# Narrow diagonal blocks share a bank in the max pass of a two-layer causal attention kernel

## The chip, the cores and the metric

The kernel runs on one core of a Trainium2 chip. The metric is the device time of one execution in microseconds (us), as the median of several runs. A core has a matrix engine (TensorE, PE in the rows), a vector engine (VectorE, DVE), an activation engine (ScalarE, ACT), GpSimd (POOL) and SyncE (SP), which work side by side and meet at semaphores. Matrix results land in PSUM, which has eight banks of 128 partitions by 512 fp32 values.

## What is computed

Two transformer layers in "macaron" form over x of 2048 tokens by 128 features, all fp32. Each layer is half an FFN, a causal attention, and the same half FFN again. The change touches the attention alone, of which there are two:

```
x = x + 0.5 * L0_ffn(layernorm(x))     # 8 experts, top 1, then a layernorm
x = x + L0_attn(layernorm(x))          # 16 heads of 8, with output projection
x = x + 0.5 * L0_ffn(layernorm(x))
x = x + 0.5 * L1_ffn(layernorm(x))     # ternary weights, relu
x = x + L1_attn(layernorm(x))          # 16 heads of 8, no output projection
x = x + 0.5 * L1_ffn(layernorm(x))

scores = einsum('bhqd,bhkd->bhqk', q, k)
scores = where(causal, scores, -inf)
attn   = softmax(scores / sqrt(8), axis=-1)
ctx    = einsum('bhqk,bhkd->bhqd', attn, v)
```

## The kernel before

**Steps and turns.** The 16 heads are taken in four groups `g` of four (`G`), the 2048 queries in four chunks `c` of 512 (`CH`). A step `(g, c)` is one group with one chunk. The 16 steps of a layer (`STEPS`) go up with groups 0 and 1, (0,0), (1,0), (0,1), ... (1,3), and down with groups 2 and 3, (2,3), (3,3), (2,2), ... (3,0). A step has 4(c+1) *quads*: four heads, 128 keys (block `j`), up to 512 queries. The last four quads of a step are *diagonal*: their queries begin at the key block, so they are 512, 384, 256 and 128 wide, and a mask is added to their first 128 columns. One quad, with some work of the max pass beside it, is a *turn*; a layer has 160 turns with a quad, 64 of them diagonal.

**The two passes.** The softmax needs each query's maximum before the exponent is taken, and the maximum is put into the score product as an added row of `q_slots`. So there is a max pass two steps ahead (`AHEAD = 2`). Its *units* are scores with queries on the partitions: block `i` of 128 queries of the chunk, key chunk `kc`, one head. TensorE multiplies (L1202), and where `kc == c` adds a causal mask on the last 128 columns (L1205). A unit with `kc < c` is 512 columns wide, one with `kc == c` (i+1)·128. VectorE takes its maximum from the bank (L1317). Units go through a ring of three PSUM banks (`RING = 3`): TensorE waits on `ring_read` for unit n-3 before unit n, and VectorE waits on `ring_full`. When a step's units are all read, VectorE joins their maxima (L1361, `neg_max`), a turn later TensorE turns them (L1210), VectorE splits them in two halves (L1334, L1336), and a DMA puts them into `q_slots`.

**One quad.** TensorE makes two score tiles of two heads each (`score_tile`, L1162, 32 rows of the array per head, four heads on four different sets of rows). Tile 0 of a quad uses the first pair of banks and tile 1 the second, so each waits for the exponent of the same tile of the quad before. In a diagonal quad two mask products (L1169) follow in each tile, on all 128 rows. ScalarE takes the exponent of a tile (L1279). One turn later TensorE multiplies with the values of the four heads (`values`, L1182, fp32, four heads on four sets of columns). The sum over a step stands in one bank, `O_BANK`; ScalarE copies it out (L1287) after the step's last values, and the next step's first values wait for that copy. Two turns later TensorE turns the result (L1225) and VectorE divides (L1344, L1348).

**The order of a turn.** It is written out in code, with `cuts = [0, 0, len(items) // 2 + len(items) // 4, len(items)]`: the quad's two score tiles, the first part of the turn's ring items (3 of 4, 1 of 3), the values of the quad before, the rest of the items. The items are units and the late work (`max`, `out`, `turned`, `project`), in that order.

**How units are dealt.** `units_beside_quads` weighs each unit as `UNIT_FIXED` plus its columns, each quad as `QUAD_FIXED` plus its columns, and gives each turn what the most pressing deadline asks. The deadline of a step's units is `SLACK = 3` turns before the step starts. The units of the first two steps run ahead of all quads.

## Time and profile before

| | us |
|---|---|
| median of 3 runs | 1314.45 (1314.13 to 1315.17) |
| the profiled execution, its time | 1314.37 |
| the profiled execution, its span | 1312.6 |
| layer 0's attention, first score tile to last values | about 203 to 643 |
| layer 1's attention | about 851 to 1280 |
| TensorE busy, whole span | 1186.3 (90%) |
| VectorE busy | 1033.5 (79%) |
| ScalarE busy | 668.8 (51%) |

The page divides the span of one execution by engine, by time and by group of instructions. "L1317" is a line of the kernel. An idle time with an arrow names what ended it. The matrix engine's rows overlap: a product of 512 columns has a row of 0.39 us, and the next one starts 0.22 us after it. So a busy TensorE isn't one at its limit, and how long a thing holds it is read from one start to the next in the timeline.

### The profile page before, as it was taken

The numbers are of one execution on the slowest core, as the hardware profiler recorded it, in microseconds if no ns is written. First come the engines' busy times: TensorE is split into PE (matmuls) and PEld (weight loads), VectorE is DVE, ScalarE is ACT, GpSimd is POOL, SyncE is SP. The second block draws the span as 40 slices with busy tenths as digits, with TensorE's granted clock in tenths as the row PEclk, the third lists the DMA queues.
The fourth block names the chain that finished last, engine by engine and source line by source line (L and its number), as shares of the span: only waits on it lengthen the run. The fifth ranks groups of instructions, "written<-read, shape, count | busy, mean of one in ns | idle before, by whom it ended". The sixth has DMA issues, their size and how long they took to land.

```text
span 1312.6 us, 21461 instructions
## 1 busy us (share of the span) xinstructions
PE 1186.3 (90%) x8293; PEld 461.7 (35%) x8293; DVE 1033.5 (79%) x2503; ACT 668.8 (51%) x861; POOL 65.3 (5%) x62
## 2 busy tenths in 40 slices
PE   1899968999999999999699979599999999999997
PEld 1455533222222222333355547232222222222336
DVE  8976487899999897875547566789999999877664
ACT  1322114555677667766332224145556667777663
POOL 5111010000000000000101000100000000000000
PEclk9999988999999999999799979799999999999999
DMA  4100141000000000000000000420000000000001
GB/s 147 33 1 1 48 121 57 1 2 1 2 1 1 2 1 1 1 1 2 1 0 1 1 0 25 146 57 1 1 2 1 1 1 1 1 1 2 1 2 33
DMA packets 23506, 23.26 MB, mean 18 GB/s; under 512 B 3134, under 2 KB 21220, under 8 KB 23404
## 3 DMA queue, kind: packets, MB, share of 16 engines
q1 hardware_dynamic: 22252, 18.73, 4.9%
q0 software_dynamic: 1152, 3.15, 0.9%
q8 instruction: 66, 1.08, 0.3%
q14 instruction: 36, 0.29, 0.1%
HBM read 13.20 MB, written 8.39 MB: 16 GB/s over the span
## 4 chain that ended last, share of the span: by engine, by line
PE 69%; DVE 25%; issue 2%; ACT 2%; DMA 1%; SPq 0%; DVEq 0%; ACTq 0%
PE psum L1182 19%; PE psum L1202 17%; DVE part_max L1317 14%; PE psum L442 9%; PE psum L1162 8%; PE psum L1169 4%; PE psum L466 2%; PE psum L898 2%; PE psum L1205 2%; PE psum L913 1%; DVE xn L167 1%; DVE norm_v L150 1%; PE psum L427 1%; DVE parts L838 1%; PE psum L1225 1%
## 5 line engine op out<-in xcount | busy, mean ns | idle before, releaser
L1317 DVE TENSOR_REDUCE part_max<-psum 128x1 f32<-128x512 f32 (+3 forms) x1280 | 703.5, 604 | 118.2 <-PE psum L1205 59.4
L1279 ACT ACTIVATE hidden<-psum 128x1024 f32<-128x1024 f32 (+3 forms) x640 | 542.4, 895 | 311.1 <-PE psum L1169 166.1
L1202 PE MATMUL psum<-k_slots,q_slots 128*128 128x512 f16 (+3 forms) x1280 | 396.8, 359 | 43.5 <-DVE part_max L1317 24.4
L1182 PE MATMUL psum<-hidden,v_aug 128*9 128x512 f32 (+3 forms) x2560 | 296.1, 535 | 0.0
L1202 PEld LDWEIGHTS psum<-k_slots,q_slots 128*128 128x128 f16 x1280 | 111.5, 97 | 402.0 <-DVE part_max L1317 320.0
L442 PE MATMUL psum<-parts,w_parts 128*128 128x512 f16 x768 | 177.6, 382 | 1.9 <-DVE parts L838 1.9
L1162 PE MATMUL psum<-q_slots,k_slots 32*128 32x512 f16 (+3 forms) x1280 | 163.9, 355 | 7.2 <-ACT hidden L1279 4.6
L1205 PE MATMUL psum<-ident_bf,later_keys 128*128 128x128 bf16 x512 | 111.0, 227 | 0.0
L442 PEld LDWEIGHTS psum<-parts,w_parts 128*128 128x128 f16 x768 | 73.2, 99 | 80.9 <-issue 3.0
L586 ACT CAST parts<-psum 128x512 f16<-128x512 f32 x64 | 37.2, 588 | 106.7 <-PE psum L427 106.7
L1162 PEld LDWEIGHTS psum<-q_slots,k_slots 32*128 32x128 f16 x1280 | 46.3, 91 | 109.4 <-issue 52.1
L1169 PE MATMUL psum<-later_keys,ident_bf 128*128 128x128 bf16 x512 | 73.8, 226 | 0.0
L1182 PEld LDWEIGHTS psum<-hidden,v_aug 128*9 128x9 f32 x2560 | 38.1, 88 | 72.3 <-issue 49.3
L838 DVE TENSOR_TENSOR parts<-parts 128x1024 f16<-128x1024 f16 x64 | 45.7, 738 | 18.3 <-ACT parts L586 18.2
L1205 PEld LDWEIGHTS psum<-ident_bf,later_keys 128*128 128x128 bf16 x512 | 51.9, 101 | 3.3 <-issue 0.3
L1169 PEld LDWEIGHTS psum<-later_keys,ident_bf 128*128 128x128 bf16 x512 | 29.2, 97 | 38.8 <-issue 27.1
L624 POOL TENSOR_TENSOR x_plus<-xn,bo_bc 128x512 f32<-128x512 f32 x8 | 13.8, 1720 | 566.1 <-DVE xn L167 527.4
L466 PE MATMUL psum<-wo_sb,hidden 128*128 128x128 f32 x256 | 33.3, 294 | 3.7 <-ACT hidden L577 3.7
L466 PEld LDWEIGHTS psum<-wo_sb,hidden 128*128 128x128 f32 x256 | 32.9, 209 | 5.6 <-ACT hidden L577 4.7
L953 POOL TENSOR_TENSOR x_plus<-x_res,fb_half 128x512 f32<-128x512 f32 x8 | 10.0, 1265 | 495.6 <-DVE xn L167 495.6
L244 ACT COPY xn_t<-psum 128x512 f32<-128x512 f32 x8 | 4.7, 587 | 58.2 <-PE psum L219 58.2
L675 DVE TENSOR_TENSOR x_plus<-psum,x_plus 128x512 f32<-128x512 f32 x8 | 5.5, 690 | 35.4 <-PE psum L466 35.4
(168 smaller groups left out, 735.7 us busy)
## 6 DMA issues: line engine op xcount, KB each, us to landing
q_slots<-q_rows SPq DMA_DIRECT2D x8, 512.0 KB, 3.8
k_slots<-k_rows POOLq DMA_DIRECT2D x24, 128.0 KB, 4.1
q_rows<-parts SPq DMA_DIRECT2D x18, 128.0 KB, 2.7
k_rows<-parts SPq DMA_DIRECT2D x18, 128.0 KB, 2.4
q_slots<-in_L_ffn_W_dram SPq DMA_DIRECT2D x2, 1024.0 KB, 6.6
k_slots<-k_rows SPq DMA_DIRECT2D x8, 128.0 KB, 4.0
q_slots<-nm_parts SPq DMA_DIRECT2D x64, 4.0 KB
out_dram<-x_res SPq DMA_DIRECT2D x4, 256.0 KB, 2.3
```

The source lines that it names most:

```text
L442: last = pe.matmul(psum[:, t, :], w1_parts[:, e, wp, t * P:(t + 1) * P], x_mask[:, k % NX, xp, :], start=(e == 0 and (wp, xp) == (0, 0)), ...
L466: last = pe.matmul(psum[:, DOWN_BANK, i * D:(i + 1) * D], hidden[:, n % 2, t, i * P:(i + 1) * P], wo2_sb[:, t, :], start=(t == 0), stop=(t ...
L586: act.copy(mask_sb[:, k % NX, :], psum[:, MASK_BANKS + k % 2, :]).then_inc(mask_ready, 1)
L838: dve.tensor_tensor(x_mask[:, k % NX, :, :], x_parts[:, n % 2, :, :], mask_sb[:, k % NX, :].rearrange("p (a t) -> p a t", a=1).broadcast_t ...
L898: last = pe.matmul(psum[:, 6 + n % 2, i * D:(i + 1) * D], hidden[:, n % 2, t, i * P:(i + 1) * P], tw2_t[:, t, :], start=(t == 0), stop=(t ...
L1162: last = pe.matmul(psum[:, S_BANKS + 2 * (tile % 2) + par, off:CH], k_slots[rows, G * g + 2 * pr + par, j * P:(j + 1) * P], q_slots[rows, ...
L1169: last = pe.matmul(psum[:, S_BANKS + 2 * (tile % 2) + par, off:off + P], ident_bf[:, :], later_keys[:, :], start=False, stop=True)
L1182: last = pe.matmul(psum[VW * h:VW * h + DH + 1, O_BANK, off:CH], v_aug[:, j, G * g + h, :], probs[:, (2 * n + h // 2) % NP, h % 2, off:CH] ...
L1202: last = pe.matmul(psum[:, bank, 0:w], q_slots[:, g, qb * P:(qb + 1) * P], k_slots[:, G * g + h, kc * CH:kc * CH + w], start=True, stop=kc ...
L1205: last = pe.matmul(psum[:, bank, i * P:w], later_keys[:, :], ident_bf[:, :], start=False, stop=True)
L1279: act.activation(probs[:, tile % NP, :, off:CH], psum[:, bank:bank + 2, off:CH], ACT.Exp, scale=scale).then_inc(exp_done, 1)
L1317: dve.tensor_reduce(dst, psum[:, bank, 0:w], axis=AX.X, op=ALU.max).then_inc(ring_read, 1)
```

## The change

Four things are done to both attentions.

1. **Units of several heads.** Where a diagonal unit is 128 wide, all four heads go side by side into one bank, and where it is 256 wide, two heads. There are then as many products as before, but one mask product for the bank (its moving operand is the identity repeated, 512 or 2x128 columns), one signal, and one maximum of VectorE with 4 or 2 results. A step has 1 + 2 + 4 + 4 = 11 diagonal units where it had 16. The units of 384 and 512 columns stay as they are.
2. **Score tiles and masks.** In a diagonal quad the four score products of both tiles come first (`score_tile`), and then the four mask products (`mask_tile`), where each tile had its masks behind it. Tile 0 is now signalled only behind tile 1's products, which still wait for the exponent of tile 1 of the quad before.
3. **The cut.** A turn's items stand half ahead of the values (rounded up) and half behind.
4. **The weights.** `UNIT_FIXED` and `QUAD_FIXED` go from 64 and 64 to 100 and 500, and a unit's columns now count its mask. The units per turn that follow, of each step:

| step | turns before | turns after |
|---|---|---|
| (0,0) | 10 8 5 3 | 7 6 5 4 |
| (1,0) | 6 5 5 2 | 5 5 4 3 |
| (0,1) | 7 7 6 5 8 4 3 3 | 6 5 5 5 4 5 4 3 |
| (1,1) | 6 6 5 5 5 4 4 3 | 5 5 5 5 5 5 4 3 |
| (0,2) | 5 7 5 6 5 5 5 5 6 5 3 2 | 4 5 5 5 5 4 5 5 4 4 4 3 |
| (1,2) | 5 6 5 4 5 4 4 4 4 4 3 2 | 4 4 4 4 4 4 4 4 4 4 3 3 |
| (0,3) | 7 4 4 5 5 4 4 5 4 4 4 4 4 4 3 2 | 4 4 4 4 4 4 4 4 4 4 4 4 4 4 3 3 |
| (1,3) | 6 4 4 6 4 4 4 5 4 4 4 4 4 3 2 2 | 4 4 3 4 4 4 4 4 4 4 4 4 4 4 2 3 |
| (2,3) | 6 4 4 6 4 4 4 4 4 4 4 4 4 3 5 2 | 4 4 3 4 4 4 4 4 4 4 3 4 4 2 3 2 |
| (3,3) | 4 5 4 4 4 3 3 3 3 3 3 5 4 3 2 2 | 3 3 4 4 4 4 3 3 4 3 3 3 3 3 3 2 |
| (2,2) | 4 3 3 4 3 3 3 3 3 5 2 1 | 3 3 3 3 3 3 3 3 3 2 2 2 |
| (3,2) | 5 3 4 4 3 3 3 6 3 4 2 1 | 3 3 3 3 3 3 3 2 2 3 2 2 |
| (2,1) | 3 3 3 3 6 3 2 1 | 3 3 2 2 2 2 2 1 |
| (3,1) | 2 2 5 4 3 2 1 1 | 2 2 2 2 2 1 1 1 |
| (2,0), (3,0) | none | none |

The diff, cut to its core:

```diff
-        UNIT_FIXED, QUAD_FIXED = 64, 64
+        UNIT_FIXED, QUAD_FIXED = 100, 500
+                for kc in range(step[1] + 1):
+                    heads = CH // unit_width(step, i, kc)
+                    units += [(step, i, kc, h, heads) for h in range(0, G, heads)]
+            return heads * (unit_width(step, i, kc) + (P if kc == step[1] else 0))
...
-                    if q in diagonal:
-                        for par in range(2):
-                            last = pe.matmul(psum[:, S_BANKS + 2 * (tile % 2) + par, off:off + P],
-                                             ident_bf[:, :], later_keys[:, :], start=False, stop=True)
+                    if q not in diagonal:
+                        last.then_inc(scores_done, 1)
+                def mask_tile(q, pr):
+                    off = first_query(q)
+                    tile = 2 * quad_no[q] + pr
+                    for par in range(2):
+                        last = pe.matmul(psum[:, S_BANKS + 2 * (tile % 2) + par, off:off + P],
+                                         ident_bf[:, :], later_keys[:, :], start=False, stop=True)
                     last.then_inc(scores_done, 1)
...
-                        last = pe.matmul(psum[:, bank, 0:w], q_slots[:, g, qb * P:(qb + 1) * P],
-                                         k_slots[:, G * g + h, kc * CH:kc * CH + w], start=True, stop=kc < c)
+                        for a in range(heads):
+                            last = pe.matmul(psum[:, bank, a * w:(a + 1) * w], q_slots[:, g, qb * P:(qb + 1) * P],
+                                             k_slots[:, G * g + h0 + a, kc * CH:kc * CH + w],
+                                             start=(a == 0), stop=(kc < c))
                         if kc == c:
-                            last = pe.matmul(psum[:, bank, i * P:w], later_keys[:, :], ident_bf[:, :],
-                                             start=False, stop=True)
+                            last = pe.matmul(diagonal_part(psum[:, bank, 0:heads * w], heads),
+                                             later_keys[:, :], repeated(ident_bf, heads), start=False, stop=True)
...
-                    cuts = [0, 0, len(items) // 2 + len(items) // 4, len(items)]
+                    half = (len(items) + 1) // 2
                     if q:
                         score_tile(q, 0)
                         score_tile(q, 1)
+                    if q in diagonal:
+                        mask_tile(q, 0)
+                        mask_tile(q, 1)
+                    for item in items[:half]:
                         ring_item(item)
                     if previous:
                         values(previous)
+                    for item in items[half:]:
                         ring_item(item)
...
-                            dve.tensor_reduce(dst, psum[:, bank, 0:w], axis=AX.X, op=ALU.max).then_inc(ring_read, 1)
+                            dve.tensor_reduce(part_max[:, step_no[s] % 2, h0:h0 + heads, i, kc],
+                                              psum[:, bank, 0:heads * w].rearrange("p (a k) -> p a k", a=heads),
+                                              axis=AX.X, op=ALU.max).then_inc(ring_read, 1)
```

TensorE, the first diagonal turn of step (0,2) in layer 0. `q_slots,k_slots` are score products, `later_keys,ident_bf` the masks of a score tile, `k_slots,q_slots` units, `ident_bf,later_keys` a unit's mask, `hidden,v_aug` values; a count stands for equal rows in a row. Before:

```order
L1162 MATMUL psum<-q_slots,k_slots 128x512 x2
L1169 MATMUL psum<-later_keys,ident_bf 128x128 x2
L1162 MATMUL psum<-q_slots,k_slots 128x512 x2
L1169 MATMUL psum<-later_keys,ident_bf 128x128 x2
L1202 MATMUL psum<-k_slots,q_slots 128x512 x4
L1182 MATMUL psum<-hidden,v_aug 9x512 x4
L1202 MATMUL psum<-k_slots,q_slots 128x128
L1205 MATMUL psum<-ident_bf,later_keys 128x128
```

After, at the same place:

```order
L1179 MATMUL psum<-q_slots,k_slots 128x512 x4
L1191 MATMUL psum<-later_keys,ident_bf 128x128 x4
L1225 MATMUL psum<-k_slots,q_slots 128x512
L1225 MATMUL psum<-k_slots,q_slots 128x128 x4
L1229 MATMUL psum<-ident_bf,later_keys 128x512
L1204 MATMUL psum<-hidden,v_aug 9x512 x4
```

The score products and the masks stand in one block each, and a block of four narrow heads has one mask of 512 columns.

TensorE, a turn without a mask near the end of the same step, the one whose items include a `max` (`ident,neg_max`). Before:

```order
L1162 MATMUL psum<-q_slots,k_slots 128x512 x4
L1202 MATMUL psum<-k_slots,q_slots 128x512 x4
L1182 MATMUL psum<-hidden,v_aug 9x512 x4
L1202 MATMUL psum<-k_slots,q_slots 128x512
L1210 MATMUL psum<-ident,neg_max 16x128
```

After:

```order
L1179 MATMUL psum<-q_slots,k_slots 128x512 x4
L1225 MATMUL psum<-k_slots,q_slots 128x512 x3
L1204 MATMUL psum<-hidden,v_aug 9x512 x4
L1225 MATMUL psum<-k_slots,q_slots 128x512 x2
L1234 MATMUL psum<-ident,neg_max 16x128
```

One unit has moved from ahead of the values to behind them.

VectorE, at the start of layer 0's attention, the units of step (0,0). Before:

```order
L276 COPY v_aug<-psum 128x64x8
L1317 TENSOR_REDUCE part_max<-psum 128x1 x16
L1361 TENSOR_REDUCE neg_max<-part_max 128x16
L141 BN_STATS norm_stats<-x_res 128x6 x4
L144 BN_AGGR norm_mean_var<-norm_stats 128x2 x4
```

After:

```order
L276 COPY v_aug<-psum 128x64x8
L1340 TENSOR_REDUCE part_max<-psum 128x4
L1340 TENSOR_REDUCE part_max<-psum 128x2 x2
L1340 TENSOR_REDUCE part_max<-psum 128x1 x8
L1386 TENSOR_REDUCE neg_max<-part_max 128x16
```

Sixteen maxima have become eleven, three of which give several results.

## Rows read from the trace of the kernel before

**Rows 1.** The page: busy time of each engine, share, instructions.
```profile
PE 1186.3 (90%) x8293; PEld 461.7 (35%) x8293; DVE 1033.5 (79%) x2503; ACT 668.8 (51%) x861; POOL 65.3 (5%) x62
```

**Rows 2.** Layer 1 by stage: us, PE, PEld, DVE, ACT, POOL busy, clock, DMA, GB/s.
```profile
851.00:878.00 27.00, 24.22 (x190) 8.58 (x189) 23.41 (x49) 11.04 (x17) 2.17 (x4) 1.00 0.26 70
878.00:929.00 51.00, 47.18 (x347) 14.69 (x347) 46.07 (x92) 27.05 (x34) 0.00 (x0) 1.00 0.01 2
929.00:1000.00 71.00, 67.22 (x473) 18.76 (x469) 65.26 (x120) 42.68 (x51) 0.00 (x0) 1.00 0.01 1
1000.00:1125.00 125.00, 122.99 (x890) 33.61 (x888) 115.80 (x213) 87.03 (x100) 0.00 (x0) 1.00 0.01 1
1125.00:1164.00 39.00, 38.25 (x282) 10.37 (x280) 32.02 (x60) 28.67 (x33) 0.00 (x0) 1.00 0.01 1
1164.00:1223.00 59.00, 58.15 (x450) 17.24 (x448) 45.91 (x90) 42.48 (x51) 0.00 (x0) 1.00 0.01 2
1223.00:1262.00 39.00, 37.33 (x318) 12.39 (x316) 24.70 (x56) 26.77 (x34) 0.00 (x0) 1.00 0.01 1
1262.00:1280.00 18.00, 16.17 (x147) 5.92 (x145) 11.34 (x57) 12.01 (x19) 2.54 (x2) 0.91 0.01 2
```

**Rows 3.** Timeline of TensorE, a turn without masks, three units: start us, us, what.
```profile
492.41 0.40 PE L1162 MATMUL psum<-q_slots,k_slots 32*128 32x512 f16 x4
492.73 0.39 PE L1202 MATMUL psum<-k_slots,q_slots 128*128 128x512 f16 x1
493.05 1.04 PE L1182 MATMUL psum<-hidden,v_aug 128*9 128x512 f32 x8
494.57 0.65 PE L1162 MATMUL psum<-q_slots,k_slots 32*128 32x512 f16 x4
```

**Rows 4.** Groups of VectorE instructions by line and shape: busy us, mean ns | idle before.
```profile
L1317 DVE TENSOR_REDUCE part_max<-psum 128x1 f32<-128x512 f32 x896 | 566.9, 684 | 75.4 <-PE psum L1202 52.4 <-PE psum L1205 18.8
L1317 DVE TENSOR_REDUCE part_max<-psum 128x1 f32<-128x256 f32 x128 | 47.5, 416 | 12.9 <-PE psum L1205 12.7
L1317 DVE TENSOR_REDUCE part_max<-psum 128x1 f32<-128x128 f32 x128 | 31.7, 285 | 15.6 <-PE psum L1205 15.1
```

**Rows 5.** Timeline of VectorE beside the turn of rows 6.
```profile
429.19 2.48 DVE L1317 TENSOR_REDUCE part_max<-psum 128x1 f32<-128x512 f32 x4 [0.47 <-PE psum L1202]
431.59 0.27 DVE L1334 TENSOR_SCALAR nm_parts<-psum 16x128 f16<-16x128 f32 x1
...
432.28 0.69 DVE L1317 TENSOR_REDUCE part_max<-psum 128x1 f32<-128x512 f32 x1
```

**Rows 6.** Timeline of TensorE, a diagonal turn of 512.
```profile
427.79 0.39 PE L1162 MATMUL psum<-q_slots,k_slots 32*128 32x512 f16 x2
428.11 0.28 PE L1169 MATMUL psum<-later_keys,ident_bf 128*128 128x128 bf16 x2
428.33 0.39 PE L1162 MATMUL psum<-q_slots,k_slots 32*128 32x512 f16 x2
428.65 0.28 PE L1169 MATMUL psum<-later_keys,ident_bf 128*128 128x128 bf16 x2
428.77 0.81 PE L1202 MATMUL psum<-k_slots,q_slots 128*128 128x512 f16 x3
429.51 1.05 PE L1182 MATMUL psum<-hidden,v_aug 128*9 128x512 f32 x8
```

**Rows 7.** Timeline of ScalarE: the exponents of rows 6's turn, and a step's copy.
```profile
428.43 1.94 ACT L1279 ACTIVATE hidden<-psum 128x1024 f32<-128x1024 f32 x2 [0.77 <-PE psum L1169]
...
481.31 0.59 ACT L1287 COPY xn_t<-psum 128x512 f32<-128x512 f32 x1
```

**Rows 8.** Timeline of TensorE, narrow values and a narrow unit.
```profile
436.76 0.62 PE L1182 MATMUL psum<-hidden,v_aug 128*9 128x256 f32 x8
437.31 0.23 PE L1202 MATMUL psum<-k_slots,q_slots 128*128 128x128 f16 x1
437.37 0.22 PE L1205 MATMUL psum<-ident_bf,later_keys 128*128 128x128 bf16 x1
```

More of the change, by code:

```diff
@@ L1009, in macaron_layers, with unit_width @@
         SLACK = 3
-        UNIT_FIXED, QUAD_FIXED = 64, 64
+        UNIT_FIXED, QUAD_FIXED = 100, 500
         def quads_of(step):
             return [(step, j) for j in range(BPC * (step[1] + 1))]
+        def unit_width(step, i, kc):
+            return CH if kc < step[1] else (i + 1) * P
         def max_units_of(step):
-            return [(step, i, kc, h) for i in range(BPC) for kc in range(step[1] + 1) for h in range(G)]
+            units = []
+            for i in range(BPC):
+                for kc in range(step[1] + 1):
+                    heads = CH // unit_width(step, i, kc)
+                    units += [(step, i, kc, h, heads) for h in range(0, G, heads)]
+            return units
         def columns_of_quad(q):
@@ L1146, in attention_layer, with diagonal_part, repeated @@
                          for s in STEPS}
+            def diagonal_part(rows, heads):
+                return rows.rearrange("p (a k) -> p a k", a=heads)[:, :, -P:]
+            def repeated(mask, heads):
+                return mask[:, :].rearrange("p (a k) -> p a k", a=1).broadcast_to([P, heads, P])
             @blk.tensor
@@ L1257, in _ @@
                         values(previous)
-                    for item in items[cuts[2]:cuts[3]]:
+                    for item in items[half:]:
                         ring_item(item)
```

18 lines of the change are left out of this document (6 added, 12 removed).

## The prediction

> **What bounds the kernel now.** The page first: TensorE is busy 1186 us of 1313, VectorE 1034 [rows 1]. Neither says which one gates the attention, so I went on to the stages [rows 2]. The eight windows are the steps of layer 1: (0,0) and (1,0); the two steps of c = 1; those of c = 2; the three of c = 3 up to (2,3); (3,3); and c = 2, 1, 0 on the way down. From 878 to 1125 TensorE and VectorE both stand above 90%; from 1125 on VectorE falls to 82%, 78% and 63% and TensorE stays at 96 to 99%. The granted clock is 1.00 but for the ends. Layer 0 has the same stages of 51, 71, 125, 39, 60 and 40 us between its ends.
>
> Then the timelines, for what holds TensorE. A turn without masks and with three units takes 2.16 us [rows 3]: 0.32 from the score products to the first unit, 0.32 from there to the values (a unit, 0.217, and 0.1 between), 0.98 for the values, and 0.54 for two units and again 0.1. So such a turn needs 1.50 us and 0.217 per unit: 2.37 with four. VectorE reads a unit of 512 in 0.60 from start to start (four in 2.48, less one row of 0.684, by three [rows 4, 5]), four in 2.4. So with four units the two are level and with three TensorE gates. In the diagonal turn [rows 6] it is different: the score products and masks take 0.98 (427.79 to 428.77) where the plain turn takes 0.32, and VectorE stands 0.47 idle beside it, ScalarE 0.77 [rows 5, 7]. That turn is TensorE's alone, and 64 of a layer's 160 are of this kind.
>
> **The change part by part.** *Masks behind both tiles.* In rows 6 a pair of 32-row products holds the array 0.213 for 512 columns, and the first row of the other kind comes 0.32 after the pair's start: 0.11 more. The two masks take 0.107, and the next score product comes 0.22 after them, again 0.11 more; the unit, which uses all rows like the masks, comes 0.12 after the second masks. So before the block is 2(0.213 + 0.11) + 0.11 + 2(0.107) = 0.97. After, all four score products run beside each other as they do in the plain turn (0.32 for four, [rows 3]), and the four masks follow: 0.213 + 0.11 + 0.213 = 0.54. That saves 0.43; with 384, 256 and 128 columns 0.38, 0.33 and 0.27, together 1.42 us per step, and for 32 steps 45 us of TensorE. The Trainium skill, page "TensorEngine Tiling (Array Packing)", section "Key Properties", says that changing the tiling mode drains the engine; the 0.11 at each change is what this trace shows of it.
>
> *Wait added.* Tile 0's signal now stands behind `score_tile(q, 1)`, which waits for the last exponent of the quad before. Queued behind it on TensorE are the masks, the units and the values; ScalarE waits for it. From the score products to the first exponent it is 0.64 us [rows 6, 7], so from now on a diagonal turn can't be shorter than its exponents plus 0.62: 1.94 + 0.62 for 512 columns, with exponents of 1.5, 1.1 and 0.8 for the narrower ones. Only in the first diagonal turn of a step (before 3.1 us, after 2.5 by TensorE) and in the c = 0 steps is that near.
>
> *Merged units.* A maximum costs VectorE its row less 0.08: 0.60 for 512, 0.335 for 256, 0.205 for 128 [rows 4, 5]. Four of 128 in one: 0.82 to 0.60. Four of 256 in two: 1.34 to 1.20. Per step 0.36 us, for 32 steps 11.5 us of VectorE. I take the several results of one maximum at no cost, since what is read stays the same; a cost above nothing eats from these 11.5. TensorE gains next to nothing: a narrow unit holds it 0.06 and its mask as much ([rows 8]: 437.31, 437.37), and columns stay what they were; I take the masks at 0.055 per head both ways. The page "Perfetto Trace Analysis" of the Trainium skill, section "Optimizing Scalar/DVE Operations", gives about 125 ns for each VectorE operation on PSUM where rows 4 show 0.072 for 285 less 0.08 less the 133 that 128 columns add. By the page the five operations saved per step would be 0.63 us, 20 us for all; since VectorE is the larger in a third of the turns, the sum would be some 3 us lower.
>
> *Cut and weights.* Both move work, and cost nothing by themselves. With 2 and 2 instead of 3 and 1 a plain turn of four units has the same 2.37. The new deal evens out turns: of (0,2) the second had seven units and the last two, now five and three.
>
> *The sum.* For each of the 160 turns I took the need of the three engines and the largest of them. TensorE: its block as above, 0.98, 0.77, 0.56 or 0.34 for the values of the quad before ([rows 6, 8]: 0.98 and 0.55, a quarter of the columns 0.21), 0.1 ahead of values and of scores, and the units. VectorE: its maxima. ScalarE: its exponents, 0.59 for a step's copy [rows 7], after the change 0.62 in diagonal turns. The late items are the same on both sides (a `max` some 0.7 of VectorE [rows 5] and 0.2 of TensorE, an `out` 0.6 and 0.53). Summed by the stages of rows 2, per layer, in us:
>
> | stage | TensorE, VectorE, sum of largest, before | after |
> |---|---|---|
> | c 0 up | 22.4, 23.1, 25.0 | 20.4, 24.3, 24.6 |
> | c 1 up | 43.6, 45.1, 49.3 | 41.2, 46.2, 46.7 |
> | c 2 up | 62.1, 63.5, 67.9 | 58.8, 61.2, 63.5 |
> | c 3, three steps | 117.3, 111.3, 120.2 | 112.8, 110.0, 117.7 |
> | (3,3) | 36.8, 30.7, 37.9 | 36.2, 32.1, 38.0 |
> | c 2 down | 54.8, 42.8, 56.8 | 51.4, 40.2, 54.0 |
> | c 1 down | 35.8, 22.4, 37.9 | 32.1, 19.8, 35.1 |
> | c 0 down | 14.6, 2.0, 16.5 | 11.8, 2.0, 16.8 |
> | layer | 387.4, 340.8, 411.5 | 364.7, 335.7, 396.5 |
>
> So 15.0 us per layer: of TensorE's 22.7, two thirds. The rest goes where VectorE is the largest (the planner now gives it more work early) and in the c = 0 steps, where ScalarE takes over. The sum of before is 411.5 where the windows of layer 1 are 429: the turns really take 1.04 to 1.06 of it, since waits meet across turns. With 1.05 it is 15.8 per layer, 31.5 for both. The profiled execution took 1314.4, beside a median of 1314.45: **1283 us**.
>
> **Rivals.** *VectorE is the floor* up to (2,3), and the holes in its diagonal turns don't close. Then these nine steps give only what its need falls, 243.0 to 241.7, and the way down 5.1: 6.4 per layer, 12.8 for both, 1302. For it speak the stages from 878 to 1125 with VectorE above 90% [rows 2], against it the hole of 0.47 just where TensorE is relieved [rows 5]. The page on tiling of the Trainium skill, section "PSUM Bottleneck", warns of just this: once the array is packed, reading PSUM may become the bound.
>
> *The four score products don't run together*, since the exponent is late and tile 1's pair comes after tile 0's. Then a block saves only 0.22 in place of 0.35 on the mean, 62% of the whole: 20 us, 1295. ScalarE's idle time of 0.77 ahead of such a block [rows 7] speaks against it.
>
> *All of TensorE's saving arrives*, as the even deal also removes old holes: 2 x 22.7 = 45, 1269.
>
> *Slower: the half cut starves VectorE.* The values hold TensorE 0.98, and the next unit needs 0.39 more until it is done [rows 6]: 1.37 us in which VectorE lives on what stands unread in the ring. Three units last 1.8, two 1.2, and one and a half 0.9. With one and a half VectorE loses 0.47 in each turn that it gates (59 of a layer): 55 us for both, less the 31: 1338. It decides from about 1.8 units unread: there the loss is 0.27 a turn and eats the gain. Against it: such a turn needs 2.37 of TensorE and 2.4 of VectorE, so the ring is mostly full when the values start.
>
> **How the numbers follow.** Forecast (1272 to 1290) 0.52; VectorE the floor, 0.15; pairs apart, 0.08; all of it, 0.14; starved, 0.07; no difference, 0.04. The range of 1264 to 1302 holds the forecast, the pairs, the nearer part of "all of it" and about all of the floor case, 0.85 in all; I keep it, since the turn sums carry an error of some us. A measurement can tell 0.2%, 2.6 us, from no change. Faster by more than that: 0.89. Within: 0.04. Slower: 0.07.
>
> **What would show it.** In a diagonal turn of 512 the first unit comes 0.54 behind the first score product (right) or more than 0.7 (pairs apart). A merged maximum of 4x128 has a row near 0.68; 0.9 or more would make the merge worth nothing. The window of the three c = 3 steps is 122 to 123 us long rather than 125, and the c = 2 steps on the way up 66 rather than 71. If VectorE is the floor, its idle time in diagonal turns is gone and TensorE waits more for the ring. If it is starved, it has an idle time in each plain turn, ended by a unit, while the values run. The forecast is wrong above all if the turns' needs don't add as the largest of three, but as an average over neighbours: by the stages' own largest needs the gain is 10 us per layer, 1294.

## The result, and the profile after

The kernel after takes 1252.82 us (median of 4 runs, 1247.76 to 1255.31), beside 1314.29 for the kernel before (4 runs, 1309.46 to 1315.17). The ratio is 0.9535, with a 95% interval of 0.9497 to 0.9572: 61.5 us less. The forecast was 1283, with a range from 1264 to 1302. So the sign was right, the gain was twice what I had summed, and the time lies below the range.

The page of the kernel after: span, then busy time of each engine with its share of the span and its instructions.

```profile
span 1245.9 us, 20984 instructions
PE 1129.6 (91%) x8133; PEld 441.8 (35%) x8133; DVE 1016.0 (82%) x2343; ACT 665.0 (53%) x861; POOL 65.8 (5%) x62
```

Beside [rows 1], TensorE's busy time has fallen by 57 us and VectorE's by 18. The same windows as [rows 2], for layer 1 of the kernel after: one row for each stage (edges, length, then PE, PEld, DVE, ACT and POOL busy in us with their instructions, granted clock, DMA share, GB/s). The edges are rounded to whole us.

```profile
811.00:838.00 27.00, 23.46 (x195) 8.60 (x193) 25.72 (x51) 12.11 (x18) 2.17 (x4) 1.00 0.26 70
838.00:885.00 47.00, 44.72 (x338) 13.71 (x336) 45.93 (x85) 26.85 (x34) 0.00 (x0) 1.00 0.01 1
885.00:949.00 64.00, 62.64 (x465) 17.89 (x461) 62.26 (x111) 42.17 (x50) 0.00 (x0) 1.00 0.01 2
949.00:1067.00 118.00, 117.19 (x866) 31.49 (x862) 113.27 (x194) 86.51 (x99) 0.00 (x0) 1.00 0.01 1
1067.00:1106.00 39.00, 38.42 (x292) 10.79 (x291) 34.36 (x58) 29.04 (x34) 0.00 (x0) 1.00 0.01 1
1106.00:1161.00 55.00, 53.93 (x431) 15.76 (x429) 43.52 (x76) 41.97 (x50) 0.00 (x0) 1.00 0.01 1
1161.00:1197.00 36.00, 34.81 (x309) 11.46 (x309) 23.02 (x43) 26.66 (x34) 0.00 (x0) 1.00 0.01 2
1197.00:1212.00 15.00, 12.29 (x139) 4.76 (x137) 10.83 (x55) 11.35 (x18) 1.98 (x2) 1.00 0.01 2
```

In the two c = 2 steps on the way up both engines are now busy 97 to 98% of the time, in the three long c = 3 steps TensorE 99% and VectorE 96%. Measured from the first exponent of a step to the first of the next, the layer 1 stages went, in us: c = 0 up 27.1 to 24.8, c = 1 up 51.2 to 47.1, c = 2 up 70.7 to 64.0, the three c = 3 steps 124.9 to 118.2, (3,3) 39.8 to 38.3, c = 2 down 58.4 to 55.6, c = 1 down 39.3 to 35.7, c = 0 down 16.1 to 14.6. The sum is 427.4 to 398.4; in layer 0 it is 437.3 to 405.6. So the attentions give 60.7 of the 61.5 us. In what follows "the attentions" is this sum of both layers from the one profiled run of each kernel, 864.7 before and 804.0 after.

**The granted clock is in these sums.** In the c = 0 steps TensorE's granted clock is not always 1.00. This is the window of the two c = 0 steps that open layer 0, in the kernel before (clock third from the end):

```profile
203.00:233.00 30.00, 27.75 (x197) 9.34 (x195) 23.94 (x50) 11.47 (x18) 2.17 (x4) 0.89 0.22 63
```

These two steps take 29.3 us, where the same steps of layer 1, whose window has 1.00 [rows 2], take 27.1. In the kernel after both layers have 1.00 there and take 24.8. At the other end of the layers the c = 0 steps went from 16.1 to 14.6 in layer 1 and from 21.2 to 19.8 in layer 0; the windows there have a clock of 0.91 and 0.86 in the kernel before, and of 1.00 and 0.92 in the kernel after. The kernel before with the new cut alone has the old order of these steps and a clock of 1.00, and takes 14.6 in layer 1. That makes 2.1, 1.5 and 1.4: an estimated 5 of the 60.7 us are a difference of the clock in the two profiled runs (the 1.4 of layer 0 counted whole, since in layer 1 these steps take the same in both orders). Of all the others, the twelve steps from (0,1) to (3,1), the granted clock is 1.00 in both kernels; they went from 384.2 to 359.0 in layer 1 and from 386.8 to 361.1 in layer 0, and a second profile of the kernel after has 359.0 and 361.1 again. So where parts are weighed against each other below, "layer 1 to (3,1)" is the better measure: its first fourteen steps, 411.3 us before and 383.8 after.

**A diagonal turn of 512**, timeline of TensorE in the kernel after (start, us, what), to lay beside [rows 6]:

```profile
407.13 0.40 PE L1179 MATMUL psum<-q_slots,k_slots 32*128 32x512 f16 x4
407.46 0.40 PE L1191 MATMUL psum<-later_keys,ident_bf 128*128 128x128 bf16 x4
407.69 0.74 PE L1225 MATMUL psum<-k_slots,q_slots 128*128 128x512 f16 x2
408.37 1.05 PE L1204 MATMUL psum<-hidden,v_aug 128*9 128x512 f32 x8
409.34 0.60 PE L1225 MATMUL psum<-k_slots,q_slots 128*128 128x512 f16 x2
409.88 0.34 PE L1179 MATMUL psum<-q_slots,k_slots 32*128 32x384 f16 x4
```

From the first score product to the first unit it is 0.56 us (407.13 to 407.69), where [rows 6] have 0.98. The turn is 2.75 long.

**The maxima**, groups of VectorE by line and shape (busy us, mean ns of one, idle before), to lay beside [rows 4]:

```profile
L1340 DVE TENSOR_REDUCE part_max<-psum 128x1 f32<-128x512 f32 x896 | 564.5, 683 | 40.7 <-PE psum L1225 21.5 <-PE psum L1229 13.1
L1340 DVE TENSOR_REDUCE part_max<-psum 128x2 f32<-128x512 f32 x64 | 42.5, 685 | 8.5 <-PE psum L1229 8.1
L1340 DVE TENSOR_REDUCE part_max<-psum 128x4 f32<-128x512 f32 x32 | 22.1, 689 | 9.6 <-PE psum L1229 9.4
```

A maximum with two or four results takes 685 or 689 ns, as one with a single result (683). What VectorE idled ahead of maxima, by what ended it (total us, times), in the kernel before:

```profile
  PE psum L1205: 59.4, 98
  PE psum L1202: 52.4, 115
```

and in the kernel after, where the mask of a unit is L1229 and the unit L1225:

```profile
  PE psum L1229: 46.5, 85
  PE psum L1225: 21.5, 65
```

111.8 us have become 68.0. I had expected nothing of this: the planner's sums know what a unit costs, and not when it stands ready.

**One turn where it can be seen.** The second turn of step (0,2) in layer 0, in the kernel before; all engines, some rows of the timeline:

```profile
285.93 0.39 PE L1162 MATMUL psum<-q_slots,k_slots 32*128 32x512 f16 x4
...
287.40 0.28 PE L1202 MATMUL psum<-k_slots,q_slots 128*128 128x256 f16 x1 [0.21 <-DVE part_max L1317]
...
288.00 0.28 PE L1202 MATMUL psum<-k_slots,q_slots 128*128 128x256 f16 x1 [0.26 <-DVE part_max L1317]
...
288.60 0.28 PE L1202 MATMUL psum<-k_slots,q_slots 128*128 128x256 f16 x1 [0.26 <-DVE part_max L1317]
...
289.20 1.05 PE L1182 MATMUL psum<-hidden,v_aug 128*9 128x512 f32 x8
...
290.60 0.69 DVE L1317 TENSOR_REDUCE part_max<-psum 128x1 f32<-128x512 f32 x1 [0.74 <-PE psum L1202]
290.93 0.10 PEld L1162 LDWEIGHTS psum<-q_slots,k_slots 32*128 32x128 f16 x4 [0.17 <-issue]
...
291.37 1.02 ACT L1279 ACTIVATE hidden<-psum 128x1024 f32<-128x1024 f32 x1 [3.07 <-PE psum L1162]
```

Six units stand ahead of the values. TensorE computes them one by one, each when VectorE has freed a bank, and the values, which wait for nothing, stand behind them until 289.20. Then the three banks hold narrow units, VectorE reads them out before the values are through, and stands idle 0.74. The next score products come 5.00 us after the last ones, and ScalarE has stood idle 3.07. The same turn of the kernel after, which the new weights give five units instead of seven:

```profile
274.37 4.94 DVE L1340 TENSOR_REDUCE part_max<-psum 128x2 f32<-128x512 f32 x8
...
274.83 0.69 PE L1179 MATMUL psum<-q_slots,k_slots 32*128 32x512 f16 x4
...
275.46 0.64 PE L1225 MATMUL psum<-k_slots,q_slots 128*128 128x512 f16 x2
...
276.30 0.39 PE L1225 MATMUL psum<-k_slots,q_slots 128*128 128x512 f16 x1 [0.21 <-DVE part_max L1340]
...
276.62 1.05 PE L1204 MATMUL psum<-hidden,v_aug 128*9 128x512 f32 x8
277.60 0.60 PE L1225 MATMUL psum<-k_slots,q_slots 128*128 128x512 f16 x2
...
278.68 0.39 PE L1179 MATMUL psum<-q_slots,k_slots 32*128 32x512 f16 x4
```

Three units ahead of the values, all of 512 columns, two behind. VectorE's eight maxima run through without a gap, and the turn is 3.85. All parts but the masks act on this turn: it takes 4.76 with the cut alone, 4.24 with the merged units alone, and 3.24 with the weights alone, which move units to other turns. So it shows how a hole comes about, and not what one part is worth.

### The profile page after: what moved, and what is told of

The parts are those of the page before. It is cut to its first block, busy times and chain, and to the rows that moved or that the text cites. A ratio compares the mean times of both kernels' runs of the same rounds, so it can differ in the third digit from the quotient of the medians.

```text
span 1245.9 us, 20984 instructions
## 1 busy us (share of the span) xinstructions
PE 1129.6 (91%) x8133; PEld 441.8 (35%) x8133; DVE 1016.0 (82%) x2343; ACT 665.0 (53%) x861; POOL 65.8 (5%) x62
## 3 DMA queue, kind: packets, MB, share of 16 engines
q8 instruction: 64, 1.05, 0.4%
## 4 chain that ended last, share of the span: by engine, by line
PE 68%; DVE 24%; ACT 3%; issue 3%; DMA 1%; SPq 0%; DVEq 0%; ACTq 0%
PE psum L1204 19%; PE psum L1225 18%; DVE part_max L1340 13%; PE psum L442 10%; PE psum L1179 7%; PE psum L466 2%; PE psum L1191 2%; ACT hidden L1303 2%; PE psum L1229 2%; PE psum L898 2%; PE psum L913 1%; DVE xn L167 1%; DVE norm_v L150 1%; PE psum L427 1%; PE psum L1249 1%
## 5 line engine op out<-in xcount | busy, mean ns | idle before, releaser
L1340 DVE TENSOR_REDUCE part_max<-psum 128x1 f32<-128x512 f32 (+3 forms) x1120 | 686.8, 668 | 75.2 <-PE psum L1229 46.5
L1225 PE MATMUL psum<-k_slots,q_slots 128*128 128x512 f16 (+3 forms) x1280 | 380.3, 357 | 27.2 <-DVE part_max L1340 10.5
L1225 PEld LDWEIGHTS psum<-k_slots,q_slots 128*128 128x128 f16 x1280 | 105.1, 97 | 362.8 <-DVE part_max L1340 283.5
L1179 PE MATMUL psum<-q_slots,k_slots 32*128 32x512 f16 (+3 forms) x1280 | 135.0, 353 | 13.8 <-ACT hidden L1303 10.6
L1229 PE MATMUL psum<-ident_bf,later_keys 128*128 128x128 bf16 (+2 forms) x352 | 88.3, 251 | 0.0
L1179 PEld LDWEIGHTS psum<-q_slots,k_slots 32*128 32x128 f16 x1280 | 38.8, 91 | 122.9 <-ACT hidden L1303 81.5
L1191 PE MATMUL psum<-later_keys,ident_bf 128*128 128x128 bf16 x512 | 51.1, 222 | 0.0
L1229 PEld LDWEIGHTS psum<-ident_bf,later_keys 128*128 128x128 bf16 x352 | 35.4, 101 | 2.3
L941 ACT ACTIVATE hidden<-psum,bias_cols 128x512 f32<-128x512 f32 x32 | 20.0, 688 | 24.4 <-PE psum L913 24.3
L577 ACT ACTIVATE hidden<-psum,unscale 128x512 f32<-128x512 f32 x32 | 19.4, 689 | 23.8 <-PE psum L452 23.8
```

Of the source, the lines that this page charges most:

```text
L1179: last = pe.matmul(psum[:, S_BANKS + 2 * (tile % 2) + par, off:CH], k_slots[rows, G * g + 2 * pr + par, j * P:(j + 1) * P], q_slots[rows, ...
L1191: last = pe.matmul(psum[:, S_BANKS + 2 * (tile % 2) + par, off:off + P], ident_bf[:, :], later_keys[:, :], start=False, stop=True)
L1225: last = pe.matmul(psum[:, bank, a * w:(a + 1) * w], q_slots[:, g, qb * P:(qb + 1) * P], k_slots[:, G * g + h0 + a, kc * CH:kc * CH + w], ...
L1229: last = pe.matmul(diagonal_part(psum[:, bank, 0:heads * w], heads), later_keys[:, :], repeated(ident_bf, heads), start=False, stop=True)
L1340: dve.tensor_reduce(part_max[:, step_no[s] % 2, h0:h0 + heads, i, kc], psum[:, bank, 0:heads * w].rearrange("p (a k) -> p a k", a=heads), ...
```

## The experiments

The change has four parts: masks behind both tiles (*masks*), merged units (*units*), half ahead of the values (*cut*), the planner's weights (*deal*). Undoing all four in the code of after gives back the order of the kernel before. Ratios are to the kernel before on the same chip, with 95% intervals; a Δ is the difference of the attentions from 864.7, unless it is said to be from after.

### One part undone

Four kernels, and the kernel after once more.

> The changed kernel itself, on the chip of the next three, so that what they undo can be read against it. All theories: about 0.953 of before, and attention stages (first score exponent to last) of 405 and 398 us as in its first trace, against 437 and 427 before.

Measured: 1253.46, 0.9553 [0.9515, 0.9591], attentions 806.1. Two profiles of one kernel are 2 us apart there, all of it in (2,0) and (3,0) of layer 0, 19.8 and 21.8 us, with more of the low clock in the longer one; every other stage agrees within 0.1.

```
u_masks:
-    score_tile(q, 0); score_tile(q, 1)
-    if q in diagonal: mask_tile(q, 0); mask_tile(q, 1)
+    score_tile(q, 0); mask_tile(q, 0) if diagonal
+    score_tile(q, 1); mask_tile(q, 1) if diagonal
```

> The changed kernel, with each score tile's masks right behind that tile again; nothing else undone. Theory 'sum of largest needs' (the predicted 15.0 us per layer are the masks' alone, 14.8 by the turn sums): the attentions get 15 us per layer longer, 30 in all, if the other 14 per layer that went came from somewhere else (theories 'deal' and 'cut'). Theory 'masks carry all' (the whole 61 us is the array's changes between 32 and 128 rows): 60 us are given back.

Measured: 1276.64, 0.9723 [0.9683, 0.9763], attentions 830.0: 24 to 26 more than after. By the sum of largest needs it would be 27.

```
u_units:
-    heads = CH // unit_width(step, i, kc)
+    heads = 1
```

> The changed kernel with one head per unit again (16 diagonal units per step, each with its own mask and maximum); the rest as changed. So far undoing the masks' place gives back 12 us per layer, the cut 4, the deal 0, of 29 to 32. Theory 'ring': a narrow unit costs more than VectorE's 0.205 us, since it goes round a ring of three banks (product, mask, signal, maximum, signal back), and the missing 13 us per layer come back here, 26 in all. Theory 'turn sums': 1.4 to 2 us per layer, 3 to 4 in all; then the missing part is an interaction of the parts.

Measured: 1272.43, 0.9704 [0.9677, 0.9732], attentions 823.7: 18 to 20 more than after. The sum gives 4.

```
u_cut:
-    half = (len(items) + 1) // 2
+    half = len(items) // 2 + len(items) // 4
```

> The changed kernel with the old cut of a turn's items (3 of 4 and 1 of 3 ahead of the values). Theory 'cut' (half and half spreads the units so that VectorE always finds one): 15 to 28 us are given back. Theory 'deal': under 5 us. The rival of the prediction, that the half cut starves VectorE, would show as a gain here.

Measured: 1263.01, 0.9621 [0.9583, 0.9659], attentions 813.4: 7 to 9 more than after. The sum gives nothing.

```
u_deal:
-    UNIT_FIXED, QUAD_FIXED = 100, 500
-    return heads * (unit_width(step, i, kc) + (P if kc == step[1] else 0))
+    UNIT_FIXED, QUAD_FIXED = 64, 64
+    return heads * unit_width(step, i, kc)
```

> The changed kernel with the old weights 64 and 64 and unit columns without masks, so that turns have 1 to 8 units again. Theory 'deal' (the holes beyond the turn sums, 22 and 13 us in before, came of turns with 5 to 8 units next to turns with 2, where TensorE waits for the ring in one and VectorE starves in the other): 20 to 28 us are given back over both layers. Theory 'cut' or 'masks carry all': under 5 us.

Measured: 1253.2, 0.9541 [0.9502, 0.9579], attentions 805.0: no difference from after.

### One part alone

Each is the kernel after with the other three parts undone.

> The kernel before with the masks of a diagonal quad behind both score tiles, and nothing else. Turn sums: 14.8 us per layer, 30 in all. If the ring's narrow units hold the turns up as theory 'ring' says, less: 20 to 25, as undoing gave.

Measured: 1280.19, 0.9762 [0.9732, 0.9791], Δ −30.5. The sum of largest needs gives −29.6. It comes from the diagonal turns: in layer 1 those with c of 1 or more sum to 108.7 in place of 121.8.

> The kernel before with the merged units alone (old deal, old cut, masks behind each tile). Theory 'ring': about 26 us less than before. Theory 'turn sums': 3 to 4 us less (VectorE's maxima 11.5 us shorter, a third of it in turns that VectorE gates).

Measured: 1288.57, 0.9831 [0.9801, 0.9861], Δ −26.1, where the sum gives −4. Idle time of VectorE ahead of maxima (total us, times), this kernel:

```profile
  PE psum L1225: 50.0, 123
  PE psum L1229: 46.9, 79
```

> The kernel before with its items half ahead of the values and half behind, and nothing else. From the undo: 7 to 9 us less. If the cut only helps beside merged units: nothing; if it starves VectorE where narrow units are not merged: slower.

Measured: 1299.73, 0.9901 [0.9874, 0.9929], Δ −15.2, where the sum gives nothing. The same view:

```profile
  PE psum L1229: 59.0, 124
  PE psum L1225: 37.2, 112
```

> The kernel before with the weights 100 and 500 and unit columns that count the mask, nothing else. From the undo (0 +- 1 us) no change. If the deal's worth is taken over by the cut and the merged units in the changed kernel, it shows here: 5 to 15 us less.

Measured: 1309.36 (10 runs), 0.9970 [0.9957, 0.9984], Δ −2.6.

So the four alone make 26.1 + 30.5 + 15.2 + 2.6 = 74.4, together 60.7, and the four undone one at a time 25 + 19 + 8 + 0 = 52. They overlap. Each Δ has the clock of its own run in it, 1.4 us in layer 1's last step for all four. Here is the same in layer 1 to (3,1), twice the difference, so as to stand for both layers. The last column has what the sum of largest needs gives for the part alone and for the part undone, all from the terms of the prediction:

| kernel | from before | kernel | from after | sum of largest needs |
|---|---|---|---|---|
| masks alone | −29.8 | masks undone | +23.5 | −30, +27 |
| units alone | −22.2 | units undone | +17.7 | −4, +4 |
| cut alone | −13.5 | cut undone | +8.5 | 0, 0 |
| weights alone | −2.6 | weights undone | −1.7 | +2, −4 |
| after | −55.1 | second profile of after | 0.0 | −31, 0 |

With the weights alone the twelve steps from (0,1) to (3,1) gain 6.9 us by the same doubling, and the c = 0 steps on the way up, at a clock of 0.94 in this profile, lose 4.2 of it.

### Where the cut acts

The cut in diagonal turns alone, on the kernel before, tells whether its gain lies where the units are narrow.

```
o_cutdiag:
+    if q in diagonal: cuts[2] = (len(items) + 1) // 2
```

> The kernel before with the half cut in diagonal turns alone. The cut alone in all turns gave 15 us in the attentions. Theory 'cover': a diagonal turn's block of scores and masks is 0.97 us, and before it only one unit stood behind the values; two now cover it, so most of the 15 is here: 10 to 15 us less. Theory 'plain turns': the gain is where the values wait for the ring in plain turns; then under 4 us.

Measured: 1308.55, 0.9963 [0.9947, 0.9978], Δ −4.9; in layer 1 to (3,1), doubled, −3.8 of the −13.5 of the cut in all turns. About 70% of the cut's gain lies in the turns without masks. Up to step (2,3) layer 1 has 28 plain turns with four units and no late work. With the cut alone their mean went from 2.56 us to 2.47, about 5 us for both layers, and my step had both at 2.37. In the same turns the values started 1.25 us behind the first score product, and 0.94 with the cut alone. By the terms of the prediction three units ahead make that 1.07 (0.32 + 3 x 0.217 + 0.1) and two make it 0.85: the wait ahead of the values was 0.18 and is 0.09, and that is the 0.09 by which the turn is shorter.

### What of the merged units acts

Three explanations of the 26 us: VectorE saves fixed time per instruction; TensorE saves masks; or a bank then holds more unread work. The first two can each be undone while the shared bank stays.

```
o_sepmax (units alone, but one maximum per head in the shared bank):
+    for a in range(heads):
+        last = dve.tensor_reduce(part_max[:, step_no[s] % 2, h0 + a, i, kc:kc + 1],
+                                 psum[:, bank, a * w:(a + 1) * w], axis=AX.X, op=ALU.max)
+    last.then_inc(ring_read, 1)
```

> The kernel before with the merged banks and one mask for each, but with a maximum of its own for every head (4 or 2 maxima read one bank, the last one gives it free). VectorE's cost is that of before. Theory 'stock' (the ring holds three units whatever their width; three narrow ones are 0.6 to 1.0 us of VectorE's work and run out while the values hold TensorE for 1.37 us, three full banks are 1.8 us and don't): most of the 26 us of the merged units alone stays, 15 to 24 us less than before. Theory 'VectorE's cost': 0 to 5 us less.

Measured: 1291.11, 0.9834 [0.9814, 0.9854], Δ −21.0. The maxima are as many as before, and most of the gain stays. The ratio is that of the merged units alone (0.9831). Of the 5 us between the two Δ, 2.3 are the last c = 0 steps of layer 0, with more of the low clock in this profile; in layer 1 to (3,1), doubled, it is −19.3 beside −22.2. So seven eighths stay, and the fewer maxima are worth 2.9 us. VectorE's idle time ahead of maxima is as low as with merged maxima:

```profile
  PE psum L1225: 46.8, 113
  PE psum L1229: 45.2, 78
```

```
o_sepmask (units alone, but one mask product per head):
+    for a in range(heads):
+        last = pe.matmul(psum[:, bank, (a + 1) * w - P:(a + 1) * w], later_keys[:, :],
+                         ident_bf[:, :], start=False, stop=(a == heads - 1))
```

> The merged units alone, but with a mask product of 128 columns for each head in the bank in place of one of 512 or 256: five more products and weight loads per step, the same columns. Theory 'stock': the same as the merged units (0.983 of before). Theory 'TensorE's masks': 10 us or more of the gain is gone.

Measured: 1285.69, 0.9798 [0.9778, 0.9818], Δ −26.0. All of the gain stays (layer 1 to (3,1), doubled: −22.0).

If narrow units harm because they stand in clusters, it should help to spread them among the full ones, on the kernel before:

```
o_spread:
+    units = [u for k, n in enumerate(narrow) for u in wide[c * k:c * (k + 1)] + [n]]
```

> The kernel before with the same 1280 units, maxima and masks, but in each step of c = 1 to 3 the 16 diagonal units don't stand in blocks of four: each is put behind c units of 512. Theory 'stock': the ring no longer holds three narrow units when the values start, 10 to 20 us less than before. Theory 'VectorE's cost': no change, since the work is the same.

Measured: 1315.2 (10 runs), 1.0015 [0.9996, 1.0035], Δ −0.4. Nothing in the whole; by stage layer 1 has c = 2 up at 68.6 in place of 70.7, and the three c = 3 steps at 126.5 in place of 124.9. VectorE's idle time ahead of maxima is 105.1 us in 217 pieces, where the kernel before has 111.8 in 213. The theory of clusters falls, and with it a forecast of "stock", which had asked for 10 to 20 us here.

A fixed cost of each passage round the ring, by itself, is no explanation either. The sixteen units of step (0,0), twelve of them narrow, run ahead of all quads, with TensorE at nothing but units. VectorE in the kernel before, layer 0:

```profile
179.77 6.58 DVE L1317 TENSOR_REDUCE part_max<-psum 128x1 f32<-128x128 f32 x16
```

Four of each width at 0.205, 0.335, 0.47 and 0.60 make 6.4, and 0.08 more for the end of the last row: the ring keeps up with narrow units as long as TensorE stays with them. The harm needs the stretches in which TensorE does something else.

### The ring itself

If the merged units act through what the ring holds, they must be worth more with a smaller one. `RING = 2` in place of 3, in the kernel before, in that with merged units alone, and in the kernel after.

> The kernel before with a ring of two banks in place of three. Theory 'stock' (what a bank holds decides how long VectorE is fed while TensorE does the values): two full units are 1.2 us against the 1.37 us of values and refill, so every turn that was level starves by some tenths; slower by 30 to 90 us. Theory 'TensorE's masks' or a fixed cost per unit on TensorE: under 10 us slower, as in turns that TensorE gates the ring isn't what holds it.

Measured: 1456.25, 1.1089 [1.1066, 1.1113], attentions 994.0. That is 143 us, far above the 30 to 90 of "stock": the direction is as it says, the size is not.

> The merged units alone, with a ring of two banks. Theory 'stock': the gain over r2_before is larger than the 26 us that it is with three banks (30 to 50), since with narrow units two banks hold 0.4 to 0.7 us. If the merge saved a fixed cost on TensorE or VectorE, the gain stays at 20 to 26.

Measured: 1410.15, 1.0754 [1.0726, 1.0782], attentions 951.8.

> The changed kernel with a ring of two banks: what the third bank is worth where all four parts are in. Theory 'stock': 30 us or more slower than the changed kernel. If the turn sums (largest of three needs) were the whole story, the ring would not matter: under 5 us.

Measured: 1374.52, 1.0469 [1.0448, 1.0489], attentions 917.4.

One bank of three is worth 143 us to the kernel before (1456.25 less the 1313.08 of the kernel before on the same chip) and 121 to the kernel after (1374.52 less the 1253.46 of after's repetition). Merged units alone gain 46 us with two banks by the medians, where they gain 24 with three, and 42 in the attentions where they gain 26. In the twelve steps from (0,1) to (3,1) of both layers, all at a clock of 1.00, it is 31.7 in place of 19.6. Idle time of VectorE ahead of maxima in the kernel before with two banks:

```profile
  PE psum L1202: 117.6, 222
  PE psum L1205: 98.2, 179
```

and in the kernel after with two banks:

```profile
  PE psum L1225: 90.2, 186
  PE psum L1229: 78.2, 130
```

The other side of the ring, TensorE's weight loads for a unit waiting for a bank (total us, times, longest), in the order before, after, before with two banks, after with two banks:

```profile
PEld psum L1202 <- DVE part_max L1317: 320.0, 619, 1.1
```
```profile
PEld psum L1225 <- DVE part_max L1340: 283.5, 510, 0.9
```
```profile
PEld psum L1202 <- DVE part_max L1317: 467.9, 818, 1.3
```
```profile
PEld psum L1225 <- DVE part_max L1340: 430.9, 761, 1.3
```

These loads run ahead of the matmuls, so their waits are mostly no loss: the units' products themselves waited 24.4, 10.5, 95.1 and 64.1 us for a bank, in the same order. With two banks both sides wait longer. With three, the change lowers both.

### Two versions that might beat both

The kernel after with the odd item behind the values (`half = len(items) // 2`):

> The changed kernel with the odd item of a turn behind the values (turns of three: one ahead, two behind). Theory 'stock': turns of three are gated by TensorE with VectorE waiting anyway, so within 3 us of the changed kernel; in turns of five two ahead instead of three leaves the ring less full, some us slower.

Measured: 1254.64, 0.9557 [0.9541, 0.9573], attentions 805.4: the same as after (in layer 1 to (3,1), doubled, 1.0 longer).

The kernel after with its 11 diagonal units of a step spread evenly among the full ones:

```
f_spread:
+    for k, n in enumerate(narrow):
+        mixed += wide[len(wide) * k // len(narrow):len(wide) * (k + 1) // len(narrow)] + [n]
```

> The changed kernel with each step's 11 diagonal units spread between its full ones. Theory 'stock': with merged units only those of 384 (0.47 us) are short, so spreading moves little, within 5 us of the changed kernel. If narrow units in a row were the harm, 5 to 10 us faster.

Measured: 1249.99 (1248.9 to 1250.25), 0.9522 [0.9506, 0.9537], attentions 800.2. That is 3 us below after's second measurement, and the intervals overlap. In layer 1 to (3,1) it is 381.4 where both profiles of after have 383.8, in layer 0 383.5 where they have 385.8 and 385.9: a gain of 4.7 us for both layers, at the edge between the two expectations. So the order of narrow units is worth a little here, though it brought nothing to the kernel before.

## Why the prediction was right, and where it was wrong

**Masks behind both tiles: right.** The block was to be 0.54 and is 0.56. The sum of largest needs with this part alone gives 29.6 us, and 30.5 came. The added wait shows where it was forecast, in the c = 0 steps. ScalarE, the exponents of two turns in the kernel after:

```profile
1204.70 1.94 ACT L1303 ACTIVATE hidden<-psum 128x1024 f32<-128x1024 f32 x2 [0.70 <-PE psum L1191]
...
1207.28 1.51 ACT L1303 ACTIVATE hidden<-psum 128x768 f32<-128x768 f32 x2 [0.17 <-PE psum L1191]
```

From the first exponent of the turn of 512 to that of the next turn it is 2.58 (forecast 1.94 + 0.62 = 2.56), and 2.29 with the cut alone, where the masks stand behind each tile. The step makes up for it in its narrow turns: at a clock of 1.00 the last two steps take 14.6 us either way. My sum has 16.8, since it adds 0.59 for a step's copy, and the copy falls into the 0.62 that ScalarE waits anyway.

**Merged maximum: right in its price, wrong in its worth.** One row of 0.689 us for four heads, where I had said 0.68 and that several results cost nothing. What VectorE saves in instructions is the gap between units alone and separate maxima: 2.9 us of 22.2 in layer 1 to (3,1), doubled, and the sum gives 4 with this part alone. The other 19 had no term in my sum.

**The cut: the step that put it at nothing is wrong.** I wrote that with 2 and 2 instead of 3 and 1 a plain turn has the same 2.37. Alone the cut gives 13 to 15 us, beside the other parts 8. The plain turn of four units took 2.56 on the mean before, so there was a hole of 0.19 in it that my step did not see. The trace has 0.18 of it ahead of the values, and half of that is gone with the cut alone. In the kernel after, the 23 plain turns of layer 1 with four units of 512 columns and no late work take 2.37 on the mean, as forecast, and with the cut undone 2.46. The reading that fits: units at the end of the first part need a bank that VectorE has yet to free (in the crowded turn at 287.40, 288.00, 288.60), and values that wait for nothing stand behind them; with fewer units ahead they start sooner. It stays a reading, since no run separates earlier values from better spaced units.

**Weights: right, near nothing.** Alone 2.6 us (a ratio of 0.9970, clear of 1), and nothing in the kernel after.

**The step that failed most is the last one, the factor of 1.05.** The sum of largest needs was 411.5 per layer before and 396.5 after. Measured are 427.4 and 398.4 in layer 1, 437.3 and 405.6 in layer 0. So the sum for the kernel after was right to 0.5% in layer 1 and 2.3% in layer 0, in part by luck, since the last c = 0 steps are 2 us too long in it and the other stages of layer 1 4 us too short; the kernel before stood 16 and 26 us over its own. I carried that distance over as a share, "since waits meet across turns", when it was the very thing that two of the four parts remove. Up to (3,1) the sum has 395.0 before and 379.7 after. Layer 1 stood 16.3 us over it before and 4.1 after; layer 0, with the c = 0 steps of before taken at layer 1's 27.1, stood 19.0 and 6.1. So 25 us of holes closed. With the 30.6 of the sum for these steps and the 5 us of the clock in the c = 0 steps that is the 60.7 measured, and holes and clock, 30 us, are nearly all of what the forecast of 31.5 lacks; for the clock I had no term. The holes are those of units and cut: alone they gain 22.2 and 13.5 where the sum has 4 and 0, while the masks alone gain what the sum says. The row was in front of me: VectorE idle 0.47 in the diagonal turn [rows 5], and 59.4 and 52.4 us ahead of maxima over the whole. I had asked of these only whether TensorE's saving closes them.

**What the distance was made of.** Shown: it depends on the ring. A bank less costs 143 us; the merged units gain 31.7 in place of 19.6 then, in the steps from (0,1) to (3,1); and seven eighths of their gain stay when the maxima don't become fewer, all of it when, in a run of its own, the masks don't. The reading that fits is stock: TensorE gives VectorE nothing for 1.37 us, values and a unit, and three banks last 3 x 0.60 = 1.8 us if they hold full units, 3 x 0.335 = 1.0 if they hold units of 256 columns, 0.6 with 128 columns. After the change every diagonal bank but that of 384 columns is a full one. Not shown is whether it is the stock in time or the smaller number of handovers: a merged unit has both, and no run here changes one without the other. Of what "stock" had forecast, separate maxima, separate masks and the merged units with two banks came true; the spread order did not (10 to 20 us asked, none came), and two banks in the kernel before cost 143 where it had 30 to 90. So the cause of the merged units' 19 us is narrowed down to what stands in the ring, and stays open beyond that.

**The rivals.** "All of TensorE's saving arrives" had the right idea, that the holes close, and too small a price: it took TensorE's need as the end, with 45 us, as though the holes of before could not give more than the parts save. "VectorE is the floor" fell: the way up to (2,3), where it was to stop the gain, was to give 1.3 us per layer and gave 2.4 + 4.0 + 6.6 + 6.7 = 19.7 in layer 1. "Pairs apart" fell with the 0.56, and "starved" with the cut alone, which should lose 55 us by it and gained 13 to 15.

**The signs I had named.** The c = 3 steps were to be 122 to 123 us and are 118.2; c = 2 up was to be 66 and is 64.0. The bare sums, without the factor, were 117.7 and 63.5.

## What to carry to other kernels

A sum of needs says how long a kernel would be without holes; compare it with the trace of before, and treat the distance as work that a change may win, not as a share that stays. Where one engine is fed through a ring while its feeder now and then leaves for a fixed time (here 1.37 us), count what the banks hold in the reader's time (1.8, 1.0 or 0.6 us) and try to fill them: filling them gave some 19 us here beyond what it saved in instructions, though why is shown only in part. And look at what work that waits for nothing stands behind: here the values started 0.31 us sooner in turns of four units with half of the ring's work behind them, and the cut alone gave 13 to 15 us. When parts of a few us are weighed by single profiles, take stages whose granted clock is the same.

## What the runs showed of the hardware

A maximum with four results over 512 columns in PSUM takes VectorE 689 ns, one with a single result 683: several results cost next to nothing. Four score products on 32 rows followed by four masks on 128 take 0.56 us, where the alternating order took 0.98, and this difference came out in the time whole (29.6 us reckoned; 29.8 measured in layer 1 to (3,1), doubled). A third PSUM bank in this ring is worth 9 to 10% of the kernel's time (143 of 1456 us, and 121 of 1375).

In layer 1 the last step, (3,0), takes 8.4 us in the kernel before and 7.0 in the kernel after. Windows of the kernel before around its middle (granted clock in the third column from the end):

```profile
1268.00:1272.00 4.00, 3.40 (x38) 1.29 (x38) 3.52 (x22) 2.89 (x5) 0.00 (x0) 1.00 0.02 4
1272.00:1275.00 3.00, 2.98 (x16) 0.98 (x14) 2.76 (x17) 1.71 (x3) 1.27 (x1) 0.62 0.00 0
1275.00:1278.00 3.00, 3.00 (x29) 1.11 (x32) 2.57 (x13) 1.60 (x4) 0.57 (x1) 0.81 0.00 0
```

For some of these 6 us the clock granted is the lower of its two levels, 1.2 in place of 2.4 GHz; the kernel after has 1.00 in all of this step. Of the other profiles, those with the masks undone in the kernel after, with the cut in diagonal turns alone, with the spread order, and of the kernel after with two banks have the slow stretch too (16.0 to 16.1 us for the last two steps); all others have not (14.6 to 14.7), among them the cut, the units and the weights alone, which have their masks behind each tile. In layer 0 every profile has some of it in (2,0) and (3,0), and two of the same kernel differ by 2.0 us there. What brings it on is open.
